# Squared attention on one core: float32 row-group scores with masked queries in place of an arrangement of bfloat16 parts

## What is computed

```python
def _L3_attn_ref(x, Wq, bq, Wk, bk, Wv, bv, Wu, bu, pos_w, ln_gamma, ln_beta, Wf, bf):
    q = jax.nn.silu(x @ Wq + bq)
    k = jax.nn.silu(x @ Wk + bk)
    v = jax.nn.silu(x @ Wv + bv)
    u = x @ Wu + bu
    idx = S - 1 + jnp.arange(S)[None, :] - jnp.arange(S)[:, None]
    rel = pos_w[idx]
    pos_attn = jnp.einsum('nm,bmd->bnd', rel, v)
    # qh, kh, vh: 4 heads of 8
    scores = jnp.einsum('bhnd,bhmd->bhnm', qh, kh) / jnp.sqrt(jnp.float32(hd))
    causal = jnp.tril(jnp.ones((S, S), dtype=bool))
    scores = jnp.where(causal[None, None], scores * scores, 0.0)
    self_attn = jnp.einsum('bhnm,bhmd->bhnd', jax.nn.silu(scores), vh)
    a = jnp.concatenate([self_attn, pos_attn], axis=-1)
    ...
    out = jax.nn.relu(u * a @ Wf + bf) + x
```

## Time and profile before

| | us |
|---|---|
| median of 3 runs | 825.33 |
| the runs | 819.68, 825.33, 829.16 |
| the profiled execution, its own time | 829.84 |
| its span, first to last instruction | 828.1 |
| granted TensorE clock, mean share of full speed | 0.884 |
| PE busy | 664.2 (80%) |
| DVE busy | 458.9 (55%) |
| ACT busy | 336.9 (41%) |
| POOL busy | 135.1 (16%) |
| the attention block's selection load issued at | 372.50 |
| last copy of its loop issued at | 504.77 |

### The profile page before, as it was taken

One profiled execution on the slowest core, in us unless ns is written; L12 is line 12 of the kernel. 1 busy time (PEld: TensorE's weight loads), 2 busy tenths in 40 slices (PEclk: granted clock), 3 DMA queues, 4 the chain that ended last, 5 costly groups with the idle time before them and its releaser, 6 DMA issues. The chain is left out here.

```text
span 828.1 us, 13768 instructions
## 1 busy us (share of the span) xinstructions
PE 664.2 (80%) x5453; PEld 386.4 (47%) x5453; DVE 458.9 (55%) x765; ACT 336.9 (41%) x594; POOL 135.1 (16%) x196
## 2 busy tenths in 40 slices
PE   0799989599489987288598998948898799889942
PEld 0434578347369975125424554423552454255310
DVE  3435932556031243795598994754585466548632
ACT  1345720340022211106298996434455245435522
POOL 1401410200000000000086771000131022013100
PEclk9999999699878897598888999868999899889967
DMA  5000020401200002600700000000000000000001
GB/s 175 3 0 1 0 27 1 156 11 27 76 2 1 1 0 59 146 1 10 153 0 2 2 2 2 0 20 8 2 2 9 2 2 2 8 1 2 1 7 54
DMA packets 24912, 20.21 MB, mean 24 GB/s; under 512 B 17545, under 2 KB 22697, under 8 KB 24202
## 3 DMA queue, kind: packets, MB, share of 16 engines
q1 hardware_dynamic: 24266, 16.88, 8.8%
q10 hardware_dynamic: 576, 2.31, 0.7%
HBM read 9.71 MB, written 2.13 MB: 14 GB/s over the span
## 5 line engine op out<-in xcount | busy, mean ns | idle before, releaser
L1737 DVE TENSOR_REDUCE R<-ps 128x4 f32<-128x1024 f32 x48 | 57.9, 1211 | 45.5 <-PE ps L1393 45.5
L1590 ACT ACTIVATE R<-ps 128x1024 f32<-128x1024 f32 x48 | 49.1, 1023 | 61.2 <-PE ps L1404 61.2
L1201 ACT ACTIVATE R<-R 128x768 f32<-128x768 f32 x64 | 60.7, 1034 | 0.0
L1520 PE MATMUL ps<-R,early 32*128 32x512 f32 x160 | 40.6, 766 | 22.5 <-PEq L1552 20.0
L1393 PE MATMUL ps<-R,tmpA 32*128 32x256 f32 x384 | 55.0, 431 | 0.0
L1404 PE MATMUL ps<-tmpA,R 32*128 32x256 f32 x384 | 52.0, 389 | 0.0
L1746 DVE RECIPROCAL R<-R 128x256 f32<-128x256 f32 x24 | 41.9, 1746 | 14.9 <-ACT R L1583 14.9
L1108 PE MATMUL ps<-R 128*32 128x256 f32 (+1 forms) x512 | 49.7, 339 | 0.5 <-ACT R L1201 0.5
L1225 POOL TENSOR_TENSOR R<-R 128x512 f32<-128x512 f32 x32 | 45.4, 1417 | 24.9 <-DVE R L1165 24.9
L1165 DVE TENSOR_TENSOR R<-ps,lasting 128x512 f32<-128x512 f32 x64 | 41.1, 684 | 4.4 <-PE ps L1091 3.3
L1404 PEld LDWEIGHTS ps<-tmpA,R 32*128 32x128 f32 x384 | 38.9, 193 | 0.7
(11 more groups left out here) (282 smaller groups left out, 1392.1 us busy)
## 6 DMA issues: line engine op xcount, KB each, us to landing
R<-z SPq DMA_DIRECT2D x16, 256.0 KB, 4.9
R<-R SPq DMA_DIRECT2D x12, 256.0 KB, 5.3
R<-in_qv SPq DMA_DIRECT2D x1, 2560.0 KB
x<-in_x SPq DMA_DIRECT2D x4, 256.0 KB, 7.1
scratch_x<-R SPq DMA_DIRECT2D x8, 128.0 KB
Q<-scratch_x SPq DMA_DIRECT2D x1, 1024.0 KB, 5.3
out<-x SPq DMA_DIRECT2D x4, 256.0 KB, 2.5
lasting<-in_lasting ACTq DMA_DIRECT2D x1, 809.0 KB
```

The costliest lines, as they stand in the source:

```text
L1201: act.activation(a, a, ACT.Silu, scale=1.0 / AHD).then_inc(act_done, 1)
L1520: pe.matmul(ps[:, w % 6, :], m.w1[p][rows, :], h[rows, k * CH:(k + 1) * CH], start=True, stop=True).then_inc(sg["z1_ready"], 1)
L1590: act.activation(m.et[:, g % 2, 2 * i:2 * i + 2, :], ps[:, 4:6, :], ACT.Exp).then_inc(sg["exp_done"], 1)
L1737: dve.tensor_reduce(m.mx[:, g, 2 * a:2 * a + 4], ps[:, a:a + 2, :].rearrange("p i (s m) -> p (i s) m", s=S), AXX, ALU.max).then_inc(sg["ma ...
```

## The change

The bfloat16 parts, their stacking and their arrangement go. The scores' operands are the float32 tiles `q` and `k_` themselves, 32 rows an image; the query tile is multiplied by a column mask `hcol` of each head into `qm`, so that the contraction over 32 rows holds that head's eight alone. A unit is now (group, head, pair of images), and its k is the image within the pair. `scores(u0)` issues both units of a pair interleaved, eight float32 matmuls over four row groups, and waits for units up to u0 - 2. `values(u0)` takes the same matmuls as before in an order that touches the four column groups in turn. The position product is done group by group at the start of a group's values, in the free half of its bank, and one copy of 512 columns (`sapa`) takes both results out. `vm` is zeroed by a memset and filled by ScalarE's copies of each head's columns, chunk 0 before the loop, the others within it, as is Silu of value chunks 1 to 3. One Silu takes the 1536 columns of two units.

```diff
-    order = [(g, hp, j) for g in range(G) for hp in range(2) for j in range(J)]
+    order = [(g, h, jp) for g in range(G) for h in range(AH) for jp in range(2)]
     NU = len(order)
+    UG = NU // G
     SLOTS = 8
     LAG = 6
...
+    def rows_of(j):
+        return slice(32 * j, 32 * j + 32)
...
+            def scores(u0):
+                g, h, _ = order[u0]
+                if u0 % (2 * UG) == 0:
+                    pe.wait_ge(q_masked, AH * (g // 2 + 1))
+                if u0 == 2:
+                    pe.wait_ge(v_biased, 2)
+                if u0 >= 2:
+                    pe.wait_ge(causal_done, u0 - 1)
+                    pe.wait_ge(below_squared, u0 - 1)
                 for s in range(S):
...
+                    at = g * N + s * 128
+                    for u in (u0, u0 + 1):
+                        for k in range(2):
+                            rows = rows_of(2 * order[u][2] + k)
+                            mm = pe.matmul(ps[:, 2 * (u % 3) + k, s * N:N + s * 128], k_[rows, at:at + 128],
+                                           m.qm[rows, h, at:(g + 1) * N], start=True, stop=True)
+                        if s == S - 1:
+                            mm.then_inc(scores_ready, 1)
+            def position(g):
+                pe.wait_ge(v_done, g // 2 + 1)
                 for s in range(S):
+                    pe.matmul(ps[:, 6 + g % 2, N:2 * N], vtok[:, (2 * g + s) * 128:(2 * g + s + 1) * 128],
+                              m.relt[:, s, :], start=(s == 0), stop=(s == S - 1))
+            def values(u0):
+                g, h, _ = order[u0]
+                if u0 % UG == 0:
+                    if g == 0:
+                        pe.wait_ge(v_biased, NCH)
+                    if g >= 2:
+                        pe.wait_ge(pv_copied, g - 1)
+                    position(g)
+                    pe.wait_ge(v_spread, AH if g < 2 else 2 * AH)
+                pe.wait_ge(act_done, u0 // 2 + 1)
+                for s in range(S):
+                    at = 0 if s == 0 else N
                     for k in range(2):
...
                         for u in (u0, u0 + 1):
-                            g, hp, j = order[u]
-                            h = 2 * hp + k
-                            at = 0 if s == 0 else N
-                            mm = pe.matmul(ps[32 * j:32 * j + 32, 6 + g % 2, s * 128:N], vm[:, (2 * g + s) * J + j, h, :],
+                            j = 2 * order[u][2] + k
+                            mm = pe.matmul(ps[rows_of(j), 6 + g % 2, s * 128:N], vm[:, (2 * g + s) * J + j, h, :],
                                            m.att[:, u % SLOTS, k, at:at + N - s * 128],
                                            start=(h == 0 and s == 0), stop=(h == AH - 1 and s == S - 1))
                             if k == 1 and s == S - 1:
                                 mm.then_inc(pv_ready, 1)
 
-            pe.wait_ge(arranged[0], len(arrangement) // 2)
-            pe.wait_ge(arranged[1], len(arrangement) // 2)
             for u in range(0, NU + LAG, 2):
                 if u < NU:
                     scores(u)
-                    scores(u + 1)
-                if u == LAG:
-                    pe.wait_ge(v_masked, 1)
                 if u >= LAG:
                     values(u - LAG)
...
+            def mask_queries(k, h):
+                if h == 0:
+                    dve.wait_ge(silu_done, k + 1)
+                c = slice(k * CH, (k + 1) * CH)
+                dve.tensor_scalar(m.qm[:, h, c], q[:, c], m.hcol[:, h:h + 1], None, ALU.mult).then_inc(q_masked, 1)
+            def copy_out(g):
+                dve.wait_ge(pv_ready, UG * (g + 1))
+                dve.tensor_copy(m.sapa[:, :, g * N:(g + 1) * N],
+                                ps[:, 6 + g % 2, :].rearrange("p (i n) -> p i n", i=2)).then_inc(pv_copied, 1)
             for k in range(NCH):
...
+                for h in range(AH):
+                    mask_queries(k, h)
+            for k in range(NCH):
+                dve.wait_ge(v_ready, k + 1)
+                dve.tensor_tensor(vtok[:, k * CH:(k + 1) * CH].rearrange("p (a d) -> p a d", d=32),
+                                  ps[:, NCH + k, :].rearrange("p (a d) -> p a d", d=32),
+                                  m.bv[:, None, :].broadcast_to([128, 16, 32]), ALU.add).then_inc(v_biased, 1)
...
+            def silu_values(k):
                 c = slice(k * CH, (k + 1) * CH)
                 act.wait_ge(v_biased, k + 1)
                 act.activation(vtok[:, c], vtok[:, c], ACT.Silu).then_inc(v_done, 1)
...
+            def silu(u0):
+                a = m.att[:, u0 % SLOTS:u0 % SLOTS + 2, :, :].rearrange("p u k n -> p (u k n)")
+                for squared in diag_squared:
+                    act.wait_ge(squared, u0 // 2 + 1)
+                act.wait_ge(below_squared, u0 + 2)
                 act.activation(a, a, ACT.Silu, scale=1.0 / AHD).then_inc(act_done, 1)
 
+            def spread_values(first, end):
+                act.wait_ge(v_done, end)
+                t = slice(4 * J * first, 4 * J * end)
+                for h in range(AH):
+                    c = slice(AHD * h, AHD * (h + 1))
+                    act.activation(vm[:, t, h, c], vtok[:, first * CH:end * CH].rearrange("p (t d) -> p t d", d=32)[:, :, c],
+                                   ACT.Copy).then_inc(v_spread, 1)
+            silu_values(0)
+            act.wait_ge(v_zeroed, 1)
+            spread_values(0, 1)
             for u in range(NU):
                 act.wait_ge(causal_done, u + 1)
                 act.activation(m.att[:, u % SLOTS, :, 128:N], ps[:, 2 * (u % 3):2 * (u % 3) + 2, 128:N],
                                ACT.Square).then_inc(below_squared, 1)
-                if u >= 2:
+                if u % 2 == 0 and u >= 2:
                     silu(u - 2)
+                if 2 <= u <= NCH:
+                    silu_values(u - 1)
+                if u == NCH + 2:
+                    spread_values(1, NCH)
             silu(NU - 2)
-            silu(NU - 1)
 
         @block.gpsimd
         def _(pool):
...
+            pool.memset(vm[:, :, :, :], 0.0).then_inc(v_zeroed, 1)
```

More of the change, by code:

```diff
@@ L1058, in _ @@
                     mm.then_inc(v_ready, 1)
-            pe.wait_ge(silu_done, 2 * NCH)
-            pe.wait_ge(v_done, NCH)
-            for g in range(G):
-                for s in range(S):
-                    mm = pe.matmul(ps[:, 4 + g // 2, (g % 2) * N:(g % 2) * N + N],
-                                   vtok[:, (2 * g + s) * 128:(2 * g + s + 1) * 128], m.relt[:, s, :],
-                                   start=(s == 0), stop=(s == S - 1))
-                if g % 2:
-                    mm.then_inc(pos_ready, 1)
@@ L1070, in _ @@
-            pe.wait_ge(v_biased, NCH)
-            pe.wait_ge(sel_made, 1)
-            pe.wait_ge(stacked, 16 * NPART * J)
-            for w, (k, j, hp, x) in enumerate(arrangement):
-                if w >= 4:
-                    pe.wait_ge(arranged[x], (w - 4) // 2 + 1)
-                pe.matmul(ps[:, w % 4, :], m.selqk[0:32 * NPART, x, hp, :],
-                          m.qkstack[0:32 * NPART, x, j, k * CH:(k + 1) * CH],
-                          start=True, stop=True).then_inc(arranged_ready, 1)
@@ L1096, in values @@
-            def values(u0):
-                g = order[u0][0]
-                if u0 % (2 * J) == 0 and g >= 2:
-                    pe.wait_ge(pv_copied, g - 1)
-                pe.wait_ge(act_done, u0 + 2)
-                for k in range(2):
-                    for s in range(S):
+            def scores(u0):
[7 more added lines that the diff above has]
+                    pe.wait_ge(below_squared, u0 - 1)
+                for s in range(S):
+                    at = g * N + s * 128
[6 more added lines that the diff above has]
+                            mm.then_inc(scores_ready, 1)
@@ L2182, in constants @@
     out["atab"] = sel
-    terms = ((0, 0, 0, 1, 1, 2), (0, 1, 2, 0, 1, 0))
-    sel = np.zeros((3, AH, AHD, 2, 2, 2, 8, AHD), f)
-    for x in range(2):
-        for h in range(AH):
-            for term, part_of in enumerate(terms[x]):
-                sel[part_of, h, :, x, h // 2, h % 2, term, :] = np.eye(AHD)
-    out["selqk"] = sel.reshape(96, 512)
     for name, first, lo in (("ol", 0, -R), ("orr", 1, -R + 8)):
@@ L2241 @@
                diagonal(a["L2_ffn_router_w"]), diagonal(wu[:, :C]), diagonal(wu[:, C:]), diagonal(wf[:C]),
-               diagonal(wf[C:]), rows(c["revop"]), rows(c["revstep"])]
+               diagonal(wf[C:]), rows(c["revop"]), rows(c["revstep"]), c["hcol"]]
     z_mats = [a["L2_attn_" + n].reshape(LAYERS * ZHEADS, 32, 32).transpose(0, 2, 1)
@@ L2248 @@
         "lasting": np.concatenate(lasting, axis=1),
[L2249 removed]
+        "gather": c["gather"], "scatter": c["scatter"], "sele": c["sele"],
         "atab": c["atab"],
```

122 lines of the change are left out of this document (17 added, 105 removed).

## The result

The changed kernel takes 785.53 us (median of 4 runs, 783.14 to 787.93), the kernel before 822.73 us beside it (4 runs, 819.68 to 829.16): ratio 0.9538, 95% interval 0.9466 to 0.961. Forecast were 798 us and 786 to 811. Ratios leave out an execution that is over 1.5% above the fastest of its kernel. The profiled execution took 786.78 us, 43.06 less than the 829.84 of the one before.

What follows compares the result with a forecast made beforehand. ScalarE was taken to bound the old loop by a little, a round trip the new. 396.6 + 70.7 + 2.6 + 2.4 + 5.9 = 478.2 against 505.19: 27.0 us gained, 798 us predicted, range 786 to 811.

Steps and rivals of the forecast that it cites:

- The preparation: Attention stage before its loop: first causal multiply at 396.6 us against 435.06, 38.4 us earlier.
- The loop: Attention loop: 2.28 us a pair, within bounds of 1.95 and 2.5; 31 x 2.28 = 70.7 us.
- The round trip: Loop: next scores wait for this pair's first causal multiply and Square; 0.85 + 1.25 = 2.10 us a pair.
- The extras of the first turns: Loop's start: 2.6 us for ScalarE's value Silus and spread copies, 2.4 us for three turns at half speed.
- Drain: Loop's end, from the last pair's first causal multiply through the last copy: 5.9 us with the gaps.
- The failed step: Behind the attention stage: same work after a barrier, so the stage's 27.0 us gain goes through.
- The range: Whole kernel: 786 to 811 us, taking in (a), (b) and 4 us of scatter between runs.
- (a): Rival, loop: lag covered, VectorE sets the pace at 1.95 us a pair, 10 us less, 788; chance 0.18.
- (b): Rival, loop: patchy TensorE clock or longer buffer lag, 2.6 us a pair, 10 us more, 808; chance 0.24.
- (c): Rival, loop: TensorE stays at 1.2 GHz, 3.8 us a pair, 47 us more, 845; chance 0.05.
- (d): Rival, loop: row groups don't overlap, scores 2.8 us for 0.76, 4 us a pair, 851; chance 0.03.
- The two rules: Skill pages on loop matmuls: 3.07 times for four row tiles (scores 0.2 us a pair more); tiling-mode changes drain TensorE.

Runs made afterwards that it cites:

- chain_act: Changed kernel plus a 128-column ScalarE copy nobody reads, ahead of each even unit's Square, on the round trip: 789.24 us (1 run).
- aside_act: Changed kernel plus the same small ScalarE copy, but behind the joined Silu, off the round trip: 790.32 us (1 run).
- unpaired: Changed kernel with a pair's scores issued unit by unit, each waiting for its own buffer: 782.28 us (4 runs), ratio 0.9459.
- chain_longer: Changed kernel plus a 128x128 VectorE copy nobody reads, ahead of each even unit's causal multiply: 801.04 us (4 runs), ratio 0.9694.
- chain_tt: Changed kernel plus a 128-column two-input VectorE multiply nobody reads, ahead of each even unit's causal multiply: 803.66 us (1 run).
- aside_tt: Changed kernel plus the same small two-input VectorE multiply, but behind VectorE's diagonal square: 811.23 us (1 run).
- after_nops: Changed kernel with 128 no-ops ahead of TensorE's first work: 785.23 us (4 runs), ratio 0.9509.

## Why the forecast was wrong

**The preparation** was right: 397.06 us for 396.6, with the multiplies at a pitch of 0.40 and GpSimd's memset of 6.93 us over at 379.85, before the projections began.

**The loop** was right in kind and nearly in size. The round trip is what a turn waits for (chain_act, aside_act): 2.21 for 2.10, because scores to causal multiply take 0.97, not 0.85 (of which 0.02 is a slip: 0.59 + 0.275 are 0.87); with the position product 2.74 for 2.8; on average 2.34 for 2.28, 1.9 us too little over 31 turns. The extras of the first turns were put too high, 5.0 us (2.6 and 2.4): 397.06 to 471.54, the last pair's causal multiply, is 74.48, and 31 turns of 2.34 are 72.5, so 2.0, and 3.0 too much: the granted clock was 1.00 in the first three turns, where half speed was forecast, and the long turns were the third and fourth. Drain 6.04 for 5.9. Together the last copy ended at 477.58 for 478.2: 28.0 us gained, 27.0 forecast. That it came so near is in part luck, as the misses of the turn and of the extras offset each other.

**The failed step** is the sentence "What follows starts behind a barrier and has the same work, so the gain goes through": it puts any change behind the stage at nothing. The work is the same, the time is not. The runs showed two things in its place. The tail is 6.3 us shorter on average, with no overlap between the two kernels' profiles, and has three or four instruction fetches fewer; its cause stays open. And the middle moves within 9 us with the granted clock of the routed steps, of which the profiled pair happened to show 9.07. For the medians, 822.73 - 785.53 = 37.2: 28.0 and 6.3 are 34.3, and 2.9 lie within the middle's scatter. With the tail and the stage's 1.0 us the forecast would have been 798 - 6 - 1 = 791; the rest is this scatter, and the median beside the changed kernel, 2.6 below the one forecast from. The range had only 4 us for scatter.

**The rivals.** (a), VectorE's pace and 788 us, comes nearest in the whole and is false: the turn is 2.34, not 1.95. unpaired shows that even with more slack it is 8.78 / 4 = 2.20. (b), 2.6 a pair: no. (c), TensorE at 1.2 GHz: the granted clock is 1.00 in the loop, with TensorE busy 84% only. (d), no overlap of row groups, with 2.8 us for the scores: no; they overlap even unit by unit, in 0.88.

**The two rules.** Scores of a pair take 0.87 us to the first value matmul, where 0.76 and 0.1 for the change of layout were forecast. By the 3.07 of "TensorE: Matmul & The Clock Gate", Part 3, in the Trainium skill it would be 0.2 more, an estimate; the trace disagrees with adding that to the pace. Set against the forecast's 2.8 us on the full array, the 0.87, which hold the start and the change of layout, are a factor of 3.2, not far from the page's. The change of layout does cost TensorE time, which a regular turn hides in its gap of 0.49 us. In the turn with three layouts TensorE has no gap, and the distances of starts (414.42, 415.28, 416.34, 417.13 in the changed kernel) are 0.86 us for scores, 1.06 for the position product and 0.79 for values, for 0.86, 1.03 and 0.90 forecast.

**What the change is made of.** From the norm's start to the first causal multiply it is now 24.10 us for 62.52, 38.4 less; the new loop gives 10.4 back, 80.52 us from the first causal multiply to the last copy's end for 70.13. The joined Silu is worth nothing, and the wait that comes with the interleaved order costs 3.7 of these 10.4.

## What to carry to other kernels

Before you cut instructions, see that the buffers leave slack, and count whose result frees each: issuing two units together under three buffers made each regular turn as long as a round trip through three engines. An operation on that round trip costs the time by which it delays the next one; beside it the same operation cost nothing (ScalarE's copy), as long as its engine had idle time. Matmuls need not be interleaved in the program to run side by side on different row groups: here issuing them unit by unit did as well, as long as no wait stood between them, so choose the order that waits least. And when a stage early in a program changes, give the forecast room for what lies behind it, even if not an instruction differs there: take the spread from several profiled executions, mark by mark, before you call a difference in one pair a gain.

## What the runs showed of the hardware

A VectorE operation with both operands in SBUF, begun while GpSimd's 1.42 us multiply ran, ended only 0.08 to 0.15 us behind it: 0.66 us for a 128x128 copy (chain_longer), 0.72 and 1.12 for a multiply of that size (chain_tt, aside_tt). One begun ahead of GpSimd's was not held: VectorE's diagonal square, with both inputs in SBUF, starts 0.13 to 0.16 us earlier and keeps its 0.68 us all 32 times (the changed kernel). The causal multiply, which reads PSUM, kept its 0.69 us beside GpSimd (413.17 in the changed kernel, where GpSimd ran from 412.32 to 413.74). ScalarE's copy of the same tile took 0.31. The Trainium skill ("GPSIMD Engine Reference", Specifications) says that the SBUF interfaces are shared, with contention for VectorE instructions "in a 2-port perf mode or with two SBUF inputs"; chain_tt and aside_tt agree, with 1.12 us in place of the 0.2 expected as the price. TensorE began a unit's matmuls on two free row groups 0.03 us behind those of the unit ahead on the other two, although four matmul instructions of that unit stood before them in the program and started 0.5 us later (unpaired, 425.79). And three instruction fetches behind the last relu went with 4.8 us (after_nops against after), four with 6.9 (before), where I had put nothing.
